# The seam between two stages of a fused spectral and graph convolution: who makes the low parts, and in which order

## The chip, the cores and the metric

The kernel runs on one core of a Trainium2 chip. The metric is the device time of one execution in microseconds; the median of a few executions is what is compared. The engines are TensorE (PE in the profile; PEld is its weight load), VectorE (DVE), ScalarE (ACT), GpSimd (POOL) and SyncE (SP), which here only issues transfers. ScalarE issues half of the transfers of the matrix. A `q` behind an engine's name in the profile means its queue, where transfers are issued.

## The reference

`x` is 4096 x 128 and `adj` is 4096 x 4096, both float32. `_layernorm` is a plain normalisation over the last axis.

```python
def _L0_gnn_ref(x, evals, evecs, t):              # evecs = adj
    t_eff = jnp.clip(t[0], 1e-08, None)
    x_spec = jnp.einsum('nk,nc->kc', evecs, x)
    coefs = jnp.exp(-evals * t_eff)[:, None]
    return jnp.einsum('nk,kc->nc', evecs, coefs * x_spec)

def _L1_gnn_ref(inputs, adj, W, b):
    adj_hat = adj + jnp.eye(N)
    deg = jnp.sum(adj_hat, axis=1, keepdims=True)
    return jnp.tanh((adj_hat / deg) @ (inputs @ W) + b)

x = _layernorm(x + _L0_gnn_ref(x, evals, adj, t), axis=-1)
x = _layernorm(x + _L1_gnn_ref(x, adj, W, b), axis=-1)
```

So the matrix is used three times: transposed for the spectrum, then for the spectral output, then for the graph product.

## The kernel before, in words

**Precision.** A product of two float32 tiles is made of three matmuls in float32r: each operand is split into a high part (a rounded copy) and a low part (the value less its high part), and high x high, high x low and low x high are summed in PSUM. Some products are instead made as one matmul in plain float32, called whole; such a step needs neither a high nor a low part of the matrix. Everywhere, ScalarE writes the high part (`hi`), and VectorE or GpSimd the low part (`lo`) by a subtraction.

**Stage 1, the spectrum (`visit1`, `chunk1`, `half1`).** The 4096 rows are eight groups of 512 (visits 0 to 7). A visit loads its rows in eight chunks `k`, each of two halves of 1024 columns, numbered `q` = 2k + h. Per half ScalarE makes `hi` (and row sums for the degrees, in `rsum`), VectorE `lo`, and TensorE does six matmuls. In the last visit (`LAST`), GpSimd makes the low parts of halves 1, 5, 9 and 13. `hi` and `lo` are rings of four slots here, six in the later stages. The eight PSUM banks hold the spectrum, and a bank pair is final after every fourth half of the last visit.

**The seam.** A bank pair `u` is copied by VectorE to `spec` (`spec_out`), turned by eight transposes on TensorE (`spectrum(u)`, `sT_done`), and scaled by `coef` as it is split. Before the change, for unit `k` (half a pair), ScalarE writes `s_hi` in four activations from PSUM, and for k of 4 and above two more that write `full`, a float32 copy of the unit's upper half; VectorE then writes `s_lo` in four operations from PSUM. `s_ready` counts the units that are done.

**Stage 2 and 3 (positions `p`).** The work is a list of 200 steps. A step is a load (2 MB, `n`), a unit, and one of two halves. The list is written by a planner: visit 0 is group 0 of the output, 16 steps from 4 loads, spectral products alone; visits 1 to 7 are the other groups, with graph products of the groups already known mixed in; visit 8 (steps from 134 on) is graph products alone. Each engine runs through the positions in the same order. At position p VectorE turns step p + 2 (`turn_step`, from the load buffer `raw` to `vt`), ScalarE makes `hi` of step p, GpSimd or VectorE `lo` of step p, and TensorE multiplies step p - 3 (`products`). `on_vector(s)` says which of the two makes a low part: in visits 0 to 2 every fourth split step goes to VectorE, in visit 8 every tenth, both by `SPLIT_COUNT`, the running number of split steps; in visits 3 to 7 it goes by the step's number. A slot of `hi`, `lo` and `vt` comes free when the step six before it is multiplied (`wait_slot`, `mm_done`).

**Loads.** There are four buffers (six in visit 8). The next load into a buffer is issued when the last step of its load is turned (`wait_buffer`, `BEFORE`): quarters 0 and 1 on SP's queue, quarters 2 and 3 on ScalarE's, where they are issued between its activations. SP also loads `x_sb` for each group, and moves the degrees out and back in (`deg_out`, `deg_in`) between two loads.

**Endings.** When a group is complete, `ending2` and `ending3` normalise it. They are spread over the next positions by `since2` and `since3`: among their pieces are `row_stats` and `mean_and_var` on VectorE and `inverse_deviation` on GpSimd, which stands in GpSimd's order between the low parts of two steps.

Of the kernel before, what the change touches and what calls it, by code (L numbers as in the profile page):

```python
# [27 lines left out]
def spectral_then_graph_conv(nc, x, adj, evals, t, W, b, out):  # L28
# [20 lines left out]
    R = 4  # L49
# [74 lines left out]
    def whole(s):  # L124

        st = STEP[s]
        return st.half == 1 and st.unit >= WHOLE_FROM and (st.visit < 3 and st.spectral or st.visit == NG)
# [16 lines left out]
    LATE_DVE = [q for q in range(PAIRS) if q % 4 != 1]  # L144

# [52 lines left out]
    with ctx:  # L198
# [22 lines left out]

        with nc.sbuf_tensor("xg_hi", [P, 2, R * C], f32r) as xg_hi, \
                nc.sbuf_tensor("xg_lo", [P, 2, R * C], f32r) as xg_lo, \
                nc.sbuf_tensor("spec", [P, 2, 2 * CW], f32) as spec, nc.sbuf_tensor("xn", [P, 2, R * C], f32) as xn, \
                nc.sbuf_tensor("rsum", [P, NG, R * NK], f32) as rsum:
# [34 lines left out]

        def acc2(g):
            return ps[:, g % 2, :]
# [28 lines left out]
        spec_out, sT_done, shi_ready, s_ready = map(sem, ("spec_out", "sT_done", "shi_ready", "s_ready"))  # L291
# [50 lines left out]
        def _(sp):  # L342
# [31 lines left out]
            for n in range(NL):  # L374
# [14 lines left out]
        def _(pool):  # L389
# [11 lines left out]
            for q in LATE_POOL:  # L401
# [4 lines left out]
                                        hi[:, q % RING1, :].bitcast(f32), ALU.subtract).then_inc(pool_lo1_ready, 1)  # L406

# [26 lines left out]
        def _(act):  # L434
# [55 lines left out]
            for i in range(NK + 4):  # L490
                if i < NK:
                    chunk1(LAST, i)
                if i >= 3 and i % 2 == 1 and i // 2 - 1 < NU:
                    wait_buffer(act, i // 2 - 1)
                    load_quarters(act, i // 2 - 1, (2, 3))
                if 0 <= (k := i - 4) < NK:
                    act.wait_ge(sT_done, k // 2 + 1)
                    if k == 0:
                        act.wait_ge(coef_ready, 1)
                    for jj in range(JB):  # L500
                        j = k * JB + jj
                        last = nc.scalar.activation(s_hi[:, j * C:(j + 1) * C], ps[:, k, jj * C:(jj + 1) * C],
                                                    ACT.Copy, scale=coef[:, k, jj:jj + 1])
                    if k >= WHOLE_FROM:
                        for jj in (2, 3):
# [392 lines left out]
```

## Time and profile before

| what | value |
|---|---|
| median of 3 runs | 627.07 us (626.67 to 628.39) |
| the profiled execution | 626.41 us, of which the span of the trace is 624.5 us |
| PE busy | 586.1 us, 94% of the span |
| DVE busy | 515.2 us, 82% |
| ACT busy | 400.6 us, 64% |
| POOL busy | 365.8 us, 59% |
| mean granted clock of TensorE | 0.981 |

Busy shares are means over stages with different limits. Matmuls overlap, so a busy TensorE is not one at its peak, and its idle stretches, or a granted clock under 1.00, are what costs. Stage 1 takes the first 194 us of the span, the seam runs from there to the first product at 206.1 us, and stages 2 and 3 take the rest.

### The profile page before, as it was taken

The numbers are of one execution on the slowest core, as the hardware profiler recorded it, in microseconds if no ns is written. First come the engines' busy times: TensorE is split into PE (matmuls) and PEld (weight loads), VectorE is DVE, ScalarE is ACT, GpSimd is POOL, SyncE is SP. The second block draws the span as 40 slices with busy tenths as digits, with TensorE's granted clock in tenths as the row PEclk, the third lists the DMA queues.
The fourth block names the chain that finished last, engine by engine and source line by source line (L and its number), as shares of the span: only waits on it lengthen the run. The fifth ranks groups of instructions, "written<-read, shape, count | busy, mean of one in ns | idle before, by whom it ended". The sixth has DMA issues, their size and how long they took to land.

```text
span 624.5 us, 8078 instructions
## 1 busy us (share of the span) xinstructions
PE 586.1 (94%) x2486; PEld 453.4 (73%) x2486; DVE 515.2 (82%) x605; ACT 400.6 (64%) x860; POOL 365.8 (59%) x210
## 2 busy tenths in 40 slices
PE   5999999999985799999999999999999979999993
PEld 5888888888874566667888888888888756656661
DVE  4899999999896999798889789597777586999992
ACT  4999999999975644545665646445454445544553
POOL 0000000000131988877999999779786879895972
PEclk9999999999998799999999999999999989999997
DMA  8999999999999899999996999387996299999201
GB/s 306 409 408 407 410 409 409 409 409 409 409 260 281 222 307 261 271 271 256 317 240 178 269 267 313 85 236 207 257 243 169 79 338 329 347 337 335 54 18 50
DMA packets 125065, 174.67 MB, mean 280 GB/s; under 512 B 6884, under 2 KB 105700, under 8 KB 125032
## 3 DMA queue, kind: packets, MB, share of 16 engines
q1 hardware_dynamic: 72608, 121.68, 59.5%
q10 hardware_dynamic: 52424, 52.58, 31.1%
q8 instruction: 17, 0.28, 0.2%
q14 instruction: 16, 0.13, 0.1%
HBM read 172.13 MB, written 2.11 MB: 279 GB/s over the span
## 4 chain that ended last, share of the span: by engine, by line
PE 78%; POOL 9%; DVE 5%; ACT 3%; issue 2%; ACTq 1%; DMA 1%; DVEq 0%
PE ps L785 13%; PE ps L787 13%; PE ps L786 13%; PE ps L761 9%; PE ps L762 9%; PE ps L763 9%; POOL lo L423 7%; PE ps L781 6%; DVE vt L616 3%; PE ps L850 1%; PE ps L853 1%; PE ps L746 1%; ACTq L336 1%; POOL rstd L415 1%; ACT hi L476 1%
## 5 line engine op out<-in xcount | busy, mean ns | idle before, releaser
L423 POOL TENSOR_TENSOR lo<-vt,hi 128x1024 fp32r<-128x1024 f32 x129 | 327.4, 2566 | 57.4 <-ACT hi L476 56.5
L616 DVE STREAM_TRANSPOSE vt<-raw 128x1024 f32<-128x1024 f32 x184 | 222.3, 1226 | 64.7 <-PE ps L787 54.4
L476 ACT ACTIVATE hi<-vt 128x1024 fp32r<-128x1024 f32 x163 | 169.8, 1061 | 110.3 <-DVE vt L616 91.8
L599 DVE TENSOR_TENSOR lo<-raw,hi 128x1024 fp32r<-128x1024 f32 x124 | 155.5, 1257 | 17.1 <-ACT hi L462 7.9
L462 ACT ACTIVATE hi<-raw 128x512 fp32r<-128x512 f32 x256 | 159.0, 624 | 5.4 <-PE ps L763 2.4
L404 POOL TENSOR_TENSOR lo<-raw,hi 128x1024 fp32r<-128x1024 f32 x4 | 10.7, 2674 | 177.0 <-ACT hi L462 177.0
L785 PE MATMUL ps<-hi,s_hi 128*128 128x512 f32 x232 | 99.0, 427 | 9.7 <-issue 5.2
L761 PE MATMUL ps<-hi,xg_hi 128*128 128x512 f32 x256 | 100.2, 392 | 2.4 <-DVE lo L599 1.8
L762 PE MATMUL ps<-lo,xg_hi 128*128 128x512 f32 x256 | 99.6, 389 | 0.0
L763 PE MATMUL ps<-hi,xg_lo 128*128 128x512 f32 x256 | 99.6, 389 | 0.0
L785 PE MATMUL ps<-hi,p_hi 128*128 128x512 f32 x206 | 89.1, 433 | 5.4 <-POOL lo L423 5.4
L786 PE MATMUL ps<-lo,s_hi 128*128 128x512 f32 x232 | 91.4, 394 | 0.0
L787 PE MATMUL ps<-hi,s_lo 128*128 128x512 f32 x232 | 91.4, 394 | 0.0
L787 PE MATMUL ps<-hi,p_lo 128*128 128x512 f32 x206 | 81.0, 393 | 0.0
L786 PE MATMUL ps<-lo,p_hi 128*128 128x512 f32 x206 | 80.9, 393 | 0.0
L781 PE MATMUL ps<-vt,full 128*128 128x512 f32 x148 | 69.5, 592 | 0.0
L623 DVE TENSOR_TENSOR lo<-vt,hi 128x1024 fp32r<-128x1024 f32 x34 | 65.3, 1920 | 1.6 <-ACT hi L476 1.6
L785 PEld LDWEIGHTS ps<-hi,s_hi 128*128 128x128 f32 x232 | 44.2, 190 | 26.1 <-issue 9.4
L761 PEld LDWEIGHTS ps<-hi,xg_hi 128*128 128x128 f32 x256 | 48.1, 188 | 13.9 <-DVE lo L599 2.3
L763 PEld LDWEIGHTS ps<-hi,xg_lo 128*128 128x128 f32 x256 | 48.1, 188 | 10.1
L762 PEld LDWEIGHTS ps<-lo,xg_hi 128*128 128x128 f32 x256 | 48.1, 188 | 9.6
L785 PEld LDWEIGHTS ps<-hi,p_hi 128*128 128x128 f32 x206 | 39.0, 189 | 21.0 <-POOL lo L423 10.2
(66 smaller groups left out, 515.9 us busy)
## 6 DMA issues: line engine op xcount, KB each, us to landing
raw<-in_adj_dram SPq DMA_DIRECT2D x63, 1024.0 KB, 14.7
raw<-in_adj_dram SPq DMA_DIRECT2D x90, 512.0 KB, 9.4
raw<-in_adj_dram ACTq DMA_DIRECT2D x88, 512.0 KB, 11.5
late_raw<-in_adj_dram SPq DMA_DIRECT2D x8, 512.0 KB, 11.3
late_raw<-in_adj_dram ACTq DMA_DIRECT2D x8, 512.0 KB, 13.5
xn<-in_x_dram SPq DMA_DIRECT2D x8, 256.0 KB, 14.4
x_sb<-in_x_dram SPq DMA_DIRECT2D x8, 256.0 KB, 13.3
out_dram<-x_sb ACTq DMA_DIRECT2D x7, 256.0 KB, 3.1
```

The source lines that it names most:

```text
L423: nc.gpsimd.tensor_tensor(lo[:, slot(p), :], vt[:, slot(p), :], hi[:, slot(p), :].bitcast(f32), ALU.subtract).then_inc(pool_lo_ready, 1)
L462: last = nc.scalar.activation(hi[:, q % RING1, e * CW:(e + 1) * CW], raw[:, k, 2 * h + e, :], ACT.Copy, accum_out=rsum[:, v, column:column ...
L476: nc.scalar.activation(hi[:, slot(s), :], vt[:, slot(s), :], ACT.Copy).then_inc(hi_ready, 1)
L599: nc.vector.tensor_tensor(lo[:, q % RING1, :], raw[:, k, 2 * h:2 * h + 2, :].rearrange("p r n -> p (r n)"), hi[:, q % RING1, :].bitcast(f3 ...
L616: nc.vector.transpose(vt[:, slot(s), :].rearrange("p (m a i) -> p m a i", m=2, a=RB), load_buffer(st.load).rearrange("p (a m e i) -> p e m ...
L761: nc.tensor.matmul(bank, xh, ah, start=first and r == 0, stop=False)
L762: nc.tensor.matmul(bank, xh, al, start=False, stop=False)
L763: last = nc.tensor.matmul(bank, xl, ah, start=False, stop=final and r == R - 1)
L781: return nc.tensor.matmul(out_t, full[:, STEP[s].unit - WHOLE_FROM, jj * C:(jj + 1) * C], vt[:, slot(s), jj * CW:(jj + 1) * CW], start=sta ...
L785: nc.tensor.matmul(out_t, vh, ah, start=start, stop=False)
L786: nc.tensor.matmul(out_t, vh, al, start=False, stop=False)
L787: return nc.tensor.matmul(out_t, vl, ah, start=False, stop=stop)
```

## The change

Seven edits, all at the seam or with an effect there:

1. `whole`: in visit 0 the second halves of all eight units are whole, not those of units 4 to 7 alone (steps 1, 3, 5 and 7 are new). This lowers `SPLIT_COUNT` of every later step by four, so in visit 8 the every-tenth rule falls on other steps: VectorE makes the low parts of steps 135, 147, 160 and 180, where it was 141, 156, 172 and 192. In visit 0 step 6 goes to VectorE, and steps 3 and 7 need no low part.
2. ScalarE's split of a unit (`split_spectrum`): four activations from PSUM write a float32 copy of the whole unit (`spectrum_full`), then one from that copy writes `s_hi`.
3. GpSimd makes `s_lo` (`spectrum_lo`) by one subtraction of 128 x 512 for each unit, from the copy and `s_hi`, in place of VectorE's four operations. Units 0 and 1 come ahead of half 13 of stage 1, units 2 and 3 ahead of step 0; units 4 to 7 after the low parts of positions 4, 6, 8 and 10, and ScalarE's splits of these units at the same positions.
4. VectorE turns steps 0 and 1 ahead of the copy of bank pair 2 (`spectrum_out(2)`), and step 2 ahead of pair 3.
5. TensorE does `spectrum(3)` after the products of steps 0 and 1, where it came ahead of all steps.
6. ScalarE's order at the end of stage 1 is written out: chunks 4 and 5 ahead of the first split, and the second quarters of loads 1 to 3 at other places.
7. `degrees()` runs at position 24 on VectorE, not at 8, and the two moves of the degrees on SP's queue stand one group of loads later.

```diff
-        return st.half == 1 and st.unit >= WHOLE_FROM and (st.visit < 3 and st.spectral or st.visit == NG)
+        if st.half == 0 or st.visit in range(3, NG):
+            return False
+        return st.visit == 0 or st.unit >= WHOLE_FROM and (st.spectral or st.visit == NG)
...
+    SPECTRUM_AFTER = {4: 4, 6: 5, 8: 6, 10: 7}
...
+        SF = {0: 0, 1: 1, 2: 2, 3: 3, 6: 4, 7: 0}
+        FULL_AT = {4: 0, 5: 1}
+        def spectrum_full(k):
+            if k in FULL_AT:
+                return full[:, 2 * FULL_AT[k]:2 * FULL_AT[k] + 2, :].rearrange("p a c -> p (a c)")
+            return sf[:, SF[k], :]
...
-                if n == 2 * NU - 1:
+                if n == 3 * NU - 1:
                     sp.wait_ge(deg_s, 3)
                     sp.dma_start(deg_by_tile, rdeg_tile[:, :, :]).then_inc(deg_out, 16)
-                if n == 3 * NU - 1:
+                if n == 4 * NU - 1:
...
+            def spectrum_lo(k):
+                pool.wait_ge(shi_ready, k + 1)
+                nc.gpsimd.tensor_tensor(s_lo[:, k * CW:(k + 1) * CW], spectrum_full(k),
+                                        s_hi[:, k * CW:(k + 1) * CW].bitcast(f32), ALU.subtract).then_inc(s_ready, 1)
+            assert LATE_POOL == [1, 5, 9, 13]
+            late_half(1)
+            late_half(5)
+            late_half(9)
+            spectrum_lo(0)
+            spectrum_lo(1)
+            late_half(13)
+            spectrum_lo(2)
+            spectrum_lo(3)
...
+                if p in SPECTRUM_AFTER:
+                    spectrum_lo(SPECTRUM_AFTER[p])
...
-            for i in range(NK + 4):
-                if i < NK:
...
+            def late_quarters(n):
+                wait_buffer(act, n)
+                load_quarters(act, n, (2, 3))
+            def split_spectrum(k):
+                act.wait_ge(sT_done, k // 2 + 1)
+                if k == 0:
+                    act.wait_ge(coef_ready, 1)
+                if k == LAST:
+                    act.wait_ge(mm_done, 2)
+                for jj in range(JB):
+                    last = nc.scalar.activation(spectrum_full(k)[:, jj * C:(jj + 1) * C], ps[:, k, jj * C:(jj + 1) * C],
+                                                ACT.Copy, scale=coef[:, k, jj:jj + 1])
+                last.then_inc(sfull_ready, 1)
+                act.wait_ge(sfull_ready, k + 1)
+                nc.scalar.activation(s_hi[:, k * CW:(k + 1) * CW], spectrum_full(k), ACT.Copy).then_inc(shi_ready, 1)
+            for k in range(NU):
+                chunk1(LAST, k)
+            late_quarters(0)
+            chunk1(LAST, 4)
+            chunk1(LAST, 5)
+            late_quarters(1)
+            split_spectrum(0)
+            split_spectrum(1)
+            chunk1(LAST, 6)
+            late_quarters(2)
+            chunk1(LAST, 7)
+            split_spectrum(2)
+            split_spectrum(3)
+            hi_step(0)
+            late_quarters(3)
+            hi_step(1)
...
+                if p in SPECTRUM_AFTER:
+                    split_spectrum(SPECTRUM_AFTER[p])
...
-            for i in range(NK + 4):
-                for h in range(2):
...
+            def spectrum_out(u):
+                dve.wait_ge(mm1_done, PAIRS * LAST + 4 * u + 4)
+                if u >= 2:
+                    dve.wait_ge(sT_done, u - 1)
+                for k in (2 * u, 2 * u + 1):
                     for e in range(2):
                         last = nc.vector.tensor_copy(
                             spec[:, u % 2, e * CW:(e + 1) * CW].rearrange("c (m q i) -> c q m i", m=JB, q=QN)
                             [:, 2 * (k % 2):2 * (k % 2) + 2],
                             ps[:, k, :].rearrange("c (q m e i) -> c e q m i", q=2, m=JB, e=2)[:, e])
-                    last.then_inc(spec_out, 1)
-                if 0 <= (k := i - 4) < NK:
...
+                last.then_inc(spec_out, 1)
+            for i in range(NK):
+                for h in range(2):
+                    if 2 * i + h in LATE_DVE:
+                        half1(LAST, i, h)
+                if i in (3, 5):
+                    spectrum_out((i - 3) // 2)
+            turn_step(0)
+            turn_step(1)
+            spectrum_out(2)
+            turn_step(2)
+            spectrum_out(3)
             turn_step(3)
...
-                if p == PAIRS // 2:
+                if p == PAIRS + PAIRS // 2:
...
-                    return nc.tensor.matmul(out_t, full[:, STEP[s].unit - WHOLE_FROM, jj * C:(jj + 1) * C],
+                    if STEP[s].spectral:
+                        columns_v = spectrum_full(STEP[s].unit)[:, 2 * C:]
+                    else:
+                        columns_v = full[:, STEP[s].unit - WHOLE_FROM, :]
+                    return nc.tensor.matmul(out_t, columns_v[:, jj * C:(jj + 1) * C],
...
-                    spectrum(k // 2 - 1)
-            spectrum(NU - 1)
...
+                if p - LAG == 1:
+                    spectrum(NU - 1)
```

## Rows read from the trace of the kernel before

**Rows 1.** Busy time by engine in four stretches (us), granted clock, DMA share, GB/s.
```profile
177.75:206.10 28.35, 16.51 (x81) 13.03 (x80) 23.13 (x52) 19.98 (x66) 7.08 (x3) 0.85 1.11 273
206.10:220.10 14.00, 11.36 (x37) 8.03 (x37) 13.93 (x15) 8.47 (x8) 13.88 (x6) 0.82 0.85 223
235.50:265.80 30.30, 28.95 (x118) 20.48 (x117) 25.38 (x29) 16.17 (x23) 25.91 (x14) 1.00 1.03 261
240.00:244.00 4.00, 4.00 (x18) 2.81 (x16) 4.00 (x8) 1.62 (x2) 2.92 (x2) 1.00 1.22 206
```

**Rows 2.** Timeline of TensorE at the seam: start, us, then idle before it.
```profile
180.16 0.50 PE L761 MATMUL ps<-hi,xg_hi 128*128 128x512 f32 x1 [1.36 <-DVE lo L599]
...
189.47 0.50 PE L761 MATMUL ps<-hi,xg_hi 128*128 128x512 f32 x1 [0.60 <-POOL lo L404]
...
198.97 0.47 PE L775 MATMUL ps<-ident,spec 128*128 128x128 f32 x1 [4.24 <-DVE spec L646]
...
206.11 0.76 PE L785 MATMUL ps<-hi,s_hi 128*128 128x512 f32 x1 [5.17 <-issue]
...
220.07 0.50 PE L785 MATMUL ps<-hi,s_hi 128*128 128x512 f32 x1 [1.66 <-POOL lo L423]
```

**Rows 3.** The chain that ended last, at the seam and in visit 0.
```profile
182.41 1.04 ACT s_hi L502 x4
183.45 2.44 ACT hi L462 x8
...
193.86 0.89 PE ps L775 x8
...
224.45 1.72 PE ps L781 x4
...
227.55 1.72 PE ps L781 x4
```

**Rows 4.** Groups by line: count, busy time and mean ns, idle before and releaser.
```profile
L423 POOL TENSOR_TENSOR lo<-vt,hi 128x1024 fp32r<-128x1024 f32 x129 | 327.4, 2566 | 57.4 <-ACT hi L476 56.5
L616 DVE STREAM_TRANSPOSE vt<-raw 128x1024 f32<-128x1024 f32 x184 | 222.3, 1226 | 64.7 <-PE ps L787 54.4 <-PE ps L781 10.0
L476 ACT ACTIVATE hi<-vt 128x1024 fp32r<-128x1024 f32 x163 | 169.8, 1061 | 110.3 <-DVE vt L616 91.8 <-PE ps L787 11.8 <-PE ps L781 3.2
L655 DVE SCALAR_TENSOR_TENSOR s_lo<-ps,coef,s_hi 128x128 fp32r<-128x128 f32 x32 | 9.0, 343 | 5.0 <-ACT full L506 4.2 <-ACT s_hi L502 0.8
L646 DVE COPY spec<-ps 128x256 f32<-128x256 f32 x16 | 5.6, 413 | 0.0
```

**Rows 5.** Timeline of GpSimd and of VectorE around 177 us.
```profile
176.64 2.38 POOL L404 TENSOR_TENSOR lo<-raw,hi 128x1024 fp32r<-128x1024 f32 x1 [3.16 <-ACT hi L462]
...
176.95 3.15 DVE L599 TENSOR_TENSOR lo<-raw,hi 128x1024 fp32r<-128x1024 f32 x1
```

**Rows 6.** Quarters 2 and 3 of loads 0 and 3: issue, and time to landing.
```profile
L336 ACTq DMA_DIRECT2D raw<-in_adj_dram x2: 338/422/505, 172.4 to 172.8; - x2
...
DMA to landing us min/median/max: 12.5/13.4/14.3
...
L336 ACTq DMA_DIRECT2D raw<-in_adj_dram x2: 318/415/512, 194.8 to 195.2; - x2
...
DMA to landing us min/median/max: 12.6/13.4/14.2
```

**Rows 7.** Timeline of TensorE and GpSimd in visit 8.
```profile
504.58 8.00 POOL L423 TENSOR_TENSOR lo<-vt,hi 128x1024 fp32r<-128x1024 f32 x3 [4.23 <-ACT hi L476]
...
507.00 0.50 PE L785 MATMUL ps<-hi,p_hi 128*128 128x512 f32 x1 [2.65 <-POOL lo L423]
...
516.64 0.50 PE L785 MATMUL ps<-hi,p_hi 128*128 128x512 f32 x1 [1.02 <-POOL lo L423]
...
580.28 0.20 POOL L412 TENSOR_TENSOR veps<-mv,eps_sb 128x4 f32<-128x4 f32 x1 [0.51 <-DVE mv L681]
...
584.38 0.50 PE L785 MATMUL ps<-hi,p_hi 128*128 128x512 f32 x1 [0.18 <-POOL lo L423]
```

More of the change, by code:

```diff
@@ L290, in spectral_then_graph_conv @@
         hi1_ready, lo1_ready, pool_lo1_ready, mm1_done = map(sem, ("hi1_ready", "lo1_ready", "pool_lo1_ready", "mm1_done"))
-        spec_out, sT_done, shi_ready, s_ready = map(sem, ("spec_out", "sT_done", "shi_ready", "s_ready"))
+        spec_out, sT_done, sfull_ready, shi_ready, s_ready = map(
+            sem, ("spec_out", "sT_done", "sfull_ready", "shi_ready", "s_ready"))
         vturned, hi_ready, lo_ready, pool_lo_ready, mm_done = map(
@@ L399, in _, with late_half @@
             pool.wait_ge(eps_ready, 1)
-            for q in LATE_POOL:
+            def late_half(q):
                 k, h = q // 2, q % 2
@@ L489, in _ @@
                 visit1(2 * d + 2, 0, d + 2)
-            for i in range(NK + 4):
-                if i < NK:
[L492 to L495, printed above, removed]
-                if 0 <= (k := i - 4) < NK:
[L497 to L505, printed above, removed]
-                            last = nc.scalar.activation(full[:, k - WHOLE_FROM, (jj - 2) * C:(jj - 1) * C],
-                                                        ps[:, k, jj * C:(jj + 1) * C], ACT.Copy,
-                                                        scale=coef[:, k, jj:jj + 1])
-                    last.then_inc(shi_ready, 1)
-                if i >= NK + 2:
-                    hi_step(i - NK - 2)
@@ L633, in _ @@
                 visit1(2 * d + 2, 0)
-            for i in range(NK + 4):
-                for h in range(2):
-                    if i < NK and 2 * i + h in LATE_DVE:
-                        half1(LAST, i, h)
-                for k in ((i - 3, i - 2) if i % 2 == 1 and 0 <= i - 3 < NK else ()):
-                    dve.wait_ge(mm1_done, PAIRS * LAST + 4 * (k // 2) + 4)
-                    u = k // 2
-                    if u >= 2:
-                        dve.wait_ge(sT_done, u - 1)
+            def spectrum_out(u):
[3 more added lines that the diff above has]
+                for k in (2 * u, 2 * u + 1):
                     for e in range(2):
@@ L649, in _ @@
                             ps[:, k, :].rearrange("c (q m e i) -> c e q m i", q=2, m=JB, e=2)[:, e])
-                    last.then_inc(spec_out, 1)
-                if 0 <= (k := i - 4) < NK:
-                    dve.wait_ge(shi_ready, k + 1)
-                    for jj in range(JB):
-                        j = k * JB + jj
-                        last = nc.vector.scalar_tensor_tensor(
-                            out=s_lo[:, j * C:(j + 1) * C], in0=ps[:, k, jj * C:(jj + 1) * C],
-                            scalar=coef[:, k, jj:jj + 1], in1=s_hi[:, j * C:(j + 1) * C].bitcast(f32),
-                            op0=ALU.mult, op1=ALU.subtract)
-                    last.then_inc(s_ready, 1)
-                if i >= NK + 1:
-                    turn_step(i - NK - 1)
+                last.then_inc(spec_out, 1)
[10 more added lines that the diff above has]
+            spectrum_out(3)
             turn_step(3)
-            assert not (whole(0) or on_vector(0) or whole(1) or on_vector(1))
+            assert not any(s in LO_BY_DVE for s in range(AHEAD))
             def degrees():
@@ L771, in spectrum @@
             def spectrum(u):
-                pe.wait_ge(spec_out, 2 * u + 2)
+                pe.wait_ge(spec_out, u + 1)
                 for c in range(2 * JB):
@@ L830, in _ @@
                 if k >= 3 and k % 2 == 1:
-                    spectrum(k // 2 - 1)
-            spectrum(NU - 1)
+                    spectrum((k - 3) // 2)
             def ending2(g, since):
```

2 lines of the change are left out of this document (1 added, 1 removed).

## The prediction, made before the change was run

> **What bounds the kernel now.** I read the busy time by stretch first: it shows where TensorE, busy 94% of the span, is not. From 177.75 to 220.10 it is busy 27.87 of 42.35 us [rows 1]: 14.5 us idle, and a granted clock of 0.85 and 0.82 on top. In the visit behind it is idle 1.35 of 30.30 us. So the seam is the one large hole. The timeline of TensorE then names what ends each gap [rows 2]: low parts of stage 1 (1.36 and 0.60 us), the copy of bank pair 3 behind VectorE's `s_lo` (4.24 us), the first low part of step 0 (5.17 us, put down to issue, though GpSimd finishes just then), and in visit 0 GpSimd (1.66 us). The first product after the 5.17 us takes 0.76 us, that after the 1.66 us 0.50 us: the long idle stretch brought TensorE to the lower of its clock levels (1.2 GHz), the short one did not. Last I read GpSimd, transfers and visit 8, since an earlier start presses on them.
>
> **Prices.** A split step or half is six matmuls: the pair of a whole and a split step recurs after 3.10 us and the whole one takes 1.72, so 1.38 is left [rows 3]. Eight transposes take 0.89, four activations from PSUM 1.04, a chunk of two halves on ScalarE 2.44 [rows 3]. A turn is 1.2, `hi` 1.04, VectorE's `s_lo` of a unit 4 x 9.0/32 = 1.1, the copy of a bank pair 4 x 5.6/16 = 1.4 [rows 4]. GpSimd's low part of 1024 columns is 2.38 when nothing disturbs it [rows 5] and 2.57 in the mean [rows 4]. Its 512-column one does not occur before: above 0.2 (128x4, [rows 7]) and below 2.38; it is half the columns, so 1.2. ScalarE's copy of 512 columns from SBUF lies between 0.5 (half of `hi`) and 1.04; with its wait for the activations ahead of it I take 0.65, so a split is 1.7.
>
> **The walk to step 0 (edits 2 to 6).** Half 8 starts at 180.16 in either kernel: VectorE's low part for it took 3.15 us in place of about 1.2, because it lay beside GpSimd's half 9 [rows 5], and both stay. Chunk 5 now fills ScalarE's idle time ahead of the first split; the two new copies take that up again, so chunk 6 still starts near 183.4. TensorE: halves 8 to 11 to 185.7, transposes to 186.6, half 12 to 188.0 with no wait; half 13's `hi` is there at 185.9, GpSimd starts when VectorE's half 12 is done (186.1) and ends 188.5, a wait of 0.5; halves 13 to 15 end at 192.6, against 189.47 + 3 x 1.38 = 193.6 now [rows 2]. VectorE: halves 14 and 15 behind GpSimd's 13, to 190.9; the two turns that are moved ahead of the copy, to 193.2; the copy of pair 2, to 194.6. TensorE thus waits 2.05 us there, a wait that the moved turns create, and ends its transposes at 195.5. Meanwhile ScalarE ends chunk 7 at 189.0, splits 2 and 3 at 192.4, `hi` of step 0 at 193.4; GpSimd's two unit lows end at 193.5 beside it, and its low part of step 0 at 195.95. Step 0 starts at 196.0 in place of 206.11.
>
> The Trainium skill (GPSIMD Engine Reference, Key points) says that GpSimd shares its SBUF interfaces with VectorE and contends with instructions of two SBUF inputs. The trace agrees by its 3.15 us. It speaks against handing more subtractions to GpSimd; I let the two wait for each other wherever they meet above.
>
> **Visit 0 (edits 1, 3, 5).** Sixteen steps are now eight pairs of 3.10, with 0.89 for the last transposes: 25.7 us. The four new whole steps cost TensorE 4 x 0.34 = 1.4, and spare GpSimd three low parts, VectorE one (and hand it step 6). GpSimd then has from 195.95: five low parts of 2.38 and four unit lows of 1.2, 16.7 us, and about 4 us in which it waits for `hi`, a split or VectorE; step 12 is ready at 216.6, as TensorE comes to it. I count two waits of 0.5. The visit ends at 196.0 + 25.7 + 1.0 = 222.7. Now it ends after the whole step at 227.55 and two more pairs, 227.55 + 1.72 + 6.20 = 235.5 [rows 3]. The difference is -12.8 us.
>
> **What is given back.**
> - Clock. The 2.05 us wait lies between 1.66 (kept) and 5.17 (lost) [rows 2]. Lost, it costs 0.18 x 14.0 = 2.5 [rows 1], less what the waits for GpSimd absorb. Half of that, less this: +0.8 (0 to 2.5).
> - Transfers. ScalarE's quarters of load 0 landed at 187.1, of load 3 at 209.4 [rows 6]: 7.4 us a load with the queues never empty. Load 3 comes some 0.9 earlier, at 208.5, and load n at 208.5 + 7.4(n-3). A step needs its load 4.7 us ahead of its products (turn, `hi`, low part). Step 20 would run at 228.2 and needs load 5 at 223.5; it lands at 223.3. Load 6 is needed at 230.1 and lands at 230.7. A visit is 30.3 long [rows 1], so step 44 would run near 274.2 and needs load 11 at 269.5; it lands at 267.7. All just in time: +1.0 (0 to 3). Behind visit 2 each step has more products, and this ends.
> - Degrees. 1.5 us on VectorE (estimate: three small operations, each under the 1.2 of a turn) go from position 8, where GpSimd is the bound, to 24, where VectorE is full (4.00 of 4.00 us) [rows 1]. They stand behind the statistics of group 0, ahead of the low part of step 26: +0.4 (0 to 1.5). The moves on SP's queue only change places: 0.
> - Visit 8. By the new count step 141 goes to GpSimd. Its queue there is 138, 139, 140 in 8.00 from 504.58, then the ending's small chain, then 142, which TensorE waits for at 516.64 [rows 7]. Four low parts undisturbed are 9.52, the chain 1.65, the next 2.38: 518.15, so +1.5. Step 147's move to VectorE relieves GpSimd only behind that. Step 180 goes to VectorE directly ahead of the statistics for which `inverse_deviation` already waits at 580.28; step 182's low part stands behind that, and TensorE for it at 584.38 [rows 7]: +1.2. Step 160 stands likewise ahead of the first row's statistics, but saves GpSimd one low part just there: +0.5. Steps 135, 156, 172 and 192 change where GpSimd or VectorE has idle time: 0; without that cover each is one low part, at most 2.4. Sum +3.2 (0 to 6).
>
> Visits 3 to 7 only shift.
>
> **Sum.** 626.41 (this execution) - 12.8 + 0.8 + 1.0 + 0.4 + 3.2 = 619.0. The median shown is 0.66 above its profiled execution: 619.7. About 1.9 us, 0.3%, is what a measurement of this kernel can tell from no change.
>
> **Rivals.**
> - All of the gain is kept: 614.3. For it: TensorE has idle time of its own in visit 8, which could be late at no price. Against: both steps in question are ones it waits for. 0.15.
> - The 512-column low part costs more. At 2.2 units 2 and 3 put step 0 off by 1.7 and step 12 comes 2.4 late in place of 0: 622.1. For it, only that a size not seen is guessed; against, the cost per column of the same operation. 0.08. The Trainium skill (GPSIMD Engine Reference, Key points) says that elementwise work is about twice as fast on VectorE; twice `s_lo`'s 1.1 would be 2.2, while twice a subtraction of 1.2 for 1024 columns fits the 2.38.
> - Transfers become the bound in visits 1 and 2. At 8.0 us a load, load 11 lands at 272.5, 3 late in place of 1: 622 to 623. 2.1 MB at the 206 GB/s of 240 to 244 is 10.2, at 261 it is 8.0 [rows 1]. 0.16.
> - The other side, slower: the same mechanism further on. Load 11 at 269.5 + 12.8 takes the whole gain, which is 9.2 us a load; with the rest given back it decides at 8.7. At 9.5 load 11 lands 15.0 late: 634. For it, the 206 GB/s; against, that stretch held the degrees' and `x_sb`'s transfers, and 7.4 is measured over three whole loads. 0.06.
> - The walk fails and step 0 starts past 202: 625 to 628. 0.07.
>
> The forecast has 0.48, its own range 617 to 622. With the rivals the range is 614 to 625. Faster: forecast, all kept, dear low parts, late transfers but the worst, 0.84; same 0.09; slower 0.07.
>
> **What would show it.** Step 0's product near 196, with one idle stretch near 2 us ahead of it; the first `stage` copy of group 0 near 222.7; GpSimd's 512-column operation near 1.2; VectorE waiting for a transfer ahead of the turns of steps 20 to 44, or not; TensorE's waits ahead of steps 142 and 182, 1.5 and 1.2 longer. It is wrong if the clock falls at 192.6 and stays down, if loads come slower than 7.6 us apart, or if visit 8 waits elsewhere.

## The result, and the profile after

The changed kernel takes **618.84 us** (median of 4 executions, 617.27 to 618.94) where the kernel before takes 626.87 (4, 625.44 to 628.39): a ratio of 0.9887 on record, 95% interval 0.9866 to 0.9907 (the quotient of the two medians, 0.9872, lies in it). The forecast was 619.7. The profiled execution took 618.76 us with a span of 616.8, against the sum's 619.0.

Busy time by stretch of the changed kernel (seam, visit 0, visit 1, then from the copy of group 7 to the end), columns as in [rows 1]:

```profile
179.22:194.30 15.08, 13.47 (x64) 10.57 (x65) 14.32 (x17) 11.85 (x35) 11.71 (x6) 1.00 1.11 332
194.30:222.49 28.19, 27.72 (x94) 16.66 (x94) 26.61 (x26) 17.63 (x32) 21.73 (x11) 1.00 1.10 333
222.49:252.85 30.36, 28.48 (x113) 20.05 (x114) 23.98 (x32) 16.30 (x24) 26.57 (x15) 1.00 0.98 294
484.23:616.80 132.57, 112.07 (x400) 71.86 (x398) 103.25 (x179) 62.19 (x97) 96.55 (x75) 0.96 0.77 217
```

From half 8 to the copy of group 0 the changed kernel takes 43.27 us, of which TensorE is idle 2.08, at a granted clock of 1.00 throughout. Between the same two points the kernel before takes 55.35 us, of which TensorE is idle 13.12, at a granted clock of 0.88 in the mean:

```profile
180.16:235.51 55.35, 42.23 (x161) 30.32 (x162) 48.30 (x76) 33.50 (x77) 32.10 (x13) 0.88 1.05 275
```

So 11.0 of the 12.1 us are idle time that is gone, and 1.0 is busy time, in which the clock and the four new whole steps pull opposite ways.

The changed kernel's timeline, with the rows that answer to [rows 2, 3]:

```profile
179.22 0.50 PE L807 MATMUL ps<-hi,xg_hi 128*128 128x512 f32 x1 [1.38 <-DVE lo L647]
...
193.11 1.09 PE L821 MATMUL ps<-ident,spec 128*128 128x128 f32 x8 [1.43 <-DVE spec L690]
...
214.37 0.50 PE L835 MATMUL ps<-hi,s_hi 128*128 128x512 f32 x1 [0.21 <-POOL lo L455]
...
218.97 1.88 PE L831 MATMUL ps<-vt,sf 128*128 128x512 f32 x4
...
222.61 0.50 PE L835 MATMUL ps<-hi,s_hi 128*128 128x512 f32 x1 [0.37 <-POOL lo L455]
...
225.93 0.50 PE L835 MATMUL ps<-hi,s_hi 128*128 128x512 f32 x1 [1.18 <-POOL lo L455]
```

The 4.24 and the 5.17 us are gone. One wait of 1.43 stands in their place, ahead of the transposes of pair 2, step 0 runs directly behind them at 194.30, and visit 0's last whole step starts at 218.97 (before 233.59). GpSimd's low parts of the units:

```profile
180.11 1.35 POOL L427 TENSOR_TENSOR s_lo<-sf,s_hi 128x512 fp32r<-128x512 f32 x1 [2.02 <-ACT s_hi L540]
181.81 1.90 POOL L427 TENSOR_TENSOR s_lo<-sf,s_hi 128x512 fp32r<-128x512 f32 x1 [0.35 <-ACT s_hi L540]
...
207.11 1.30 POOL L427 TENSOR_TENSOR s_lo<-sf,s_hi 128x512 fp32r<-128x512 f32 x1
```

1.30 us undisturbed, where 1.2 was assumed. The rows at 180.11 and 181.81 lie on either side of a low part on VectorE:

```profile
180.23 2.31 DVE L647 TENSOR_TENSOR lo<-raw,hi 128x1024 fp32r<-128x1024 f32 x1
```

GpSimd's first one began 0.12 us ahead of it and took 1.35, close to its undisturbed time; VectorE's took 2.31 where 1.2 is usual, and ended 1.08 us after GpSimd's had. GpSimd's next one began inside VectorE's and took 1.90, ending 1.17 us after it. So here the two take turns, and the one that starts second pays. The same holds for the 3.15 us of [rows 5]: GpSimd's began first and kept its 2.38.

The whole span by checkpoints, the starts of ScalarE's copy to `stage` of a finished group (it waits for the group's last product):

| us | half 8 | group 0 | group 1 | group 2 | group 7 | group 7 to the end of the span |
|---|---|---|---|---|---|---|
| before | 180.16 | 235.51 | 266.17 | 301.20 | 497.52 | 126.98 |
| after | 179.22 | 222.49 | 252.85 | 287.89 | 484.23 | 132.57 |
| difference | -0.94 | -13.02 | -13.32 | -13.31 | -13.29 | +5.59 |

The 0.94 us ahead of half 8 lies in a stage that the change barely touches, and this start differs from execution to execution: it is 178.43 to 180.01 us in the variants below that have the new seam, and 179.70 in the one with the old. So copies are best compared from half 8. From there the seam gained 12.1 us at group 0 and 12.4 at groups 1 and 7, and visit 8 gave 5.6 back. One more measure of noise is needed below: seven kernels (the changed one and six variants) are the same code up to group 7, and from half 8 to the copy of group 0 their traces take 42.27 to 43.58 us, to that of group 1 73.23 to 74.19.

In visit 8 TensorE and its suppliers look like this, to be set beside [rows 7]:

```profile
494.19 0.50 PE L835 MATMUL ps<-hi,p_hi 128*128 128x512 f32 x1 [3.14 <-POOL lo L455]
...
505.20 0.50 PE L835 MATMUL ps<-hi,p_hi 128*128 128x512 f32 x1 [2.31 <-POOL lo L455]
...
542.28 0.50 PE L835 MATMUL ps<-hi,p_hi 128*128 128x512 f32 x1 [1.58 <-POOL lo L455]
549.62 0.50 PE L835 MATMUL ps<-hi,p_hi 128*128 128x512 f32 x1 [0.86 <-POOL lo L455]
576.71 0.50 PE L835 MATMUL ps<-hi,p_hi 128*128 128x512 f32 x1 [0.35 <-POOL lo L455]
```

```profile
491.77 9.41 POOL L455 TENSOR_TENSOR lo<-vt,hi 128x1024 fp32r<-128x1024 f32 x4 [5.89 <-ACT hi L510]
...
538.21 0.20 POOL L444 TENSOR_TENSOR veps<-mv,eps_sb 128x4 f32<-128x4 f32 x1 [2.38 <-DVE mv L727]
...
572.62 0.20 POOL L444 TENSOR_TENSOR veps<-mv,eps_sb 128x4 f32<-128x4 f32 x1 [3.26 <-DVE mv L727]
```

GpSimd now has four low parts in a row (x4, 9.41) where it had three (x3, 8.00), and then the ending's chain. It waits 2.38 and 3.26 us for the mean (`mv`), since VectorE has a low part of its own directly ahead of the statistics. The first of the two:

```profile
534.28 2.63 DVE L671 TENSOR_TENSOR lo<-vt,hi 128x1024 fp32r<-128x1024 f32 x1
536.84 0.88 DVE L721 BATCH_NORM_STATS2 stats<-ps 128x6 f32<-128x128 f32 x4
537.75 0.38 DVE L727 BATCH_NORM_AGGREGATE mv<-stats 128x2 f32<-128x6 f32 x4
```

### The profile page after: what moved, and what is told of

The parts are those of the page before. It is cut to its first block, busy times and chain, and to the rows that moved or that the text cites. A ratio compares the mean times of both kernels' runs of the same rounds, so it can differ in the third digit from the quotient of the medians.

```text
span 616.8 us, 8026 instructions
## 1 busy us (share of the span) xinstructions
PE 584.1 (95%) x2478; PEld 448.7 (73%) x2478; DVE 509.7 (83%) x572; ACT 398.4 (65%) x856; POOL 366.6 (59%) x215
## 4 chain that ended last, share of the span: by engine, by line
PE 79%; DVE 8%; POOL 6%; ACT 2%; ACTq 2%; issue 2%; DMA 1%; DVEq 0%
PE ps L835 14%; PE ps L837 13%; PE ps L836 13%; PE ps L807 9%; PE ps L809 9%; PE ps L808 9%; PE ps L831 7%; POOL lo L455 5%; DVE vt L664 3%; ACTq L353 2%; DVE lo L647 1%; PE ps L898 1%; PE ps L901 1%; PE ps L792 1%; POOL rstd L447 1%
## 5 line engine op out<-in xcount | busy, mean ns | idle before, releaser
L455 POOL TENSOR_TENSOR lo<-vt,hi 128x1024 fp32r<-128x1024 f32 x126 | 317.1, 2541 | 46.8 <-ACT hi L510 46.2
L510 ACT ACTIVATE hi<-vt 128x1024 fp32r<-128x1024 f32 x159 | 165.1, 1060 | 105.9 <-DVE vt L664 87.9
L647 DVE TENSOR_TENSOR lo<-raw,hi 128x1024 fp32r<-128x1024 f32 x124 | 157.6, 1276 | 16.9 <-ACT hi L496 8.7
L835 PE MATMUL ps<-hi,s_hi 128*128 128x512 f32 x224 | 95.1, 425 | 3.1 <-POOL lo L455 2.6
L837 PE MATMUL ps<-hi,s_lo 128*128 128x512 f32 x224 | 87.5, 391 | 0.0
L836 PE MATMUL ps<-lo,s_hi 128*128 128x512 f32 x224 | 87.4, 390 | 0.0
L671 DVE TENSOR_TENSOR lo<-vt,hi 128x1024 fp32r<-128x1024 f32 x33 | 67.1, 2034 | 0.0
L831 PE MATMUL ps<-vt,full 128*128 128x512 f32 x124 | 59.1, 600 | 0.0
L835 PEld LDWEIGHTS ps<-hi,s_hi 128*128 128x128 f32 x224 | 42.1, 188 | 19.7 <-POOL lo L455 8.1
## 6 DMA issues: line engine op xcount, KB each, us to landing
x_sb<-in_x_dram SPq DMA_DIRECT2D x8, 256.0 KB, 13.7
```

What stands on the lines that cost most here:

```text
L510: nc.scalar.activation(hi[:, slot(s), :], vt[:, slot(s), :], ACT.Copy).then_inc(hi_ready, 1)
L647: nc.vector.tensor_tensor(lo[:, q % RING1, :], raw[:, k, 2 * h:2 * h + 2, :].rearrange("p r n -> p (r n)"), hi[:, q % RING1, :].bitcast(f3 ...
L831: return nc.tensor.matmul(out_t, columns_v[:, jj * C:(jj + 1) * C], vt[:, slot(s), jj * CW:(jj + 1) * CW], start=start, stop=stop)
L835: nc.tensor.matmul(out_t, vh, ah, start=start, stop=False)
L836: nc.tensor.matmul(out_t, vh, al, start=False, stop=False)
L837: return nc.tensor.matmul(out_t, vl, ah, start=False, stop=stop)
```

## The experiments

Twelve variants, all timed beside the kernel before. Its medians on the four occasions were 625.03, 625.27, 625.05 and 625.15 us. Most variants start from the changed kernel with VectorE's steps of visit 8 put back to 141, 156, 172, 192, called **base** below; the steps are given by this line, `SPLIT_COUNT[s] % 10 == 0` in both kernels:

```diff
-            return SPLIT_COUNT[s] % 10 == 0
+            return s in (141, 156, 172, 192)
```

**1. Who makes which low part of visit 8.** The base, from the changed kernel:

> The changed kernel, but in visit 8 VectorE makes the low parts of steps 141, 156, 172 and 192 again, as in the kernel before. Theory: the 5.6 us that the changed kernel loses again behind group 7 come from the new deal of low parts, and the lower clock after 505 us from the longer wait that it makes there; then 613.0 to 614.5 us, and the copies of groups 0 to 7 unchanged. Rival 1: they come from the changed phase of the transfers that ScalarE issues at 486 us; then 617 us or more. Rival 2: only the two waits that were forecast (1.5 and 1.2 us) go: 616 us.

Median 615.25 us (5 executions, 612.28 to 615.9), ratio 0.9828 (0.9800 to 0.9856). Group 0's copy is at 222.41 as in the changed kernel, and group 7 to the end takes 129.24 us in place of 132.57: 3.3 of the 5.6 us come back. The time lies between the theory's range and the rival's 616. It spreads, too: two of the five executions took 612.28 and 613.14, two to three microseconds less than the one that was profiled, so 3.3 is a low figure. Three variants below that have the same deal and issue their transfers at the same places in this stretch take 128.0 to 128.2 us there, which is 4.4 to 4.6 back.

The same by itself: the kernel before, its seam untouched, with the steps of the changed kernel (135, 147, 160, 180):

> The kernel before, with only its deal of low parts in visit 8 changed to steps 135, 147, 160 and 180. Theory: the deal alone costs 4.5 to 6 us wherever the seam lies: 631.5 to 633 us. Rival: it costs that only with the changed kernel's phase of transfers: 627 to 629 us.

Median 631.76 (4, 629.97 to 631.84), ratio 1.0099 (1.0074 to 1.0124). Group 7 is at 497.10, as before, and the rest takes 132.9 us in place of 126.98. So the new deal alone costs 5.9 us where nothing else is changed, as the theory had it. TensorE waits 2.31 us for step 142, the very wait of the changed kernel, and 1.66 us at the row behind step 160.

A deal that puts VectorE's parts early, `s in (139, 141, 156, 158)`, from the changed kernel:

> The changed kernel, but in visit 8 VectorE makes the low parts of steps 139, 141, 156 and 158. Theory: GpSimd reaches the ending's small chain and step 142 one low part earlier than with the old deal, and step 162's low part waits for no other: 2 to 3 us under deal_old, 611 to 612.5 us. Rival: VectorE's low part 139 waits for GpSimd's 138 and the gain is under 0.5 us.

Median 616.89 (4, 616.54 to 617.71), ratio 0.9875 (0.9853 to 0.9897): far from the 611 to 612.5 expected, and no better than the base. With one low part fewer ahead of the ending GpSimd is through at 497.6, but the mean comes only at 500.5, and TensorE then waits 2.74 us at 504.62 for what follows the chain:

```profile
500.54 0.20 POOL L444 TENSOR_TENSOR veps<-mv,eps_sb 128x4 f32<-128x4 f32 x1 [2.90 <-DVE mv L727]
```

In the base VectorE's part of step 141 stands directly ahead of `mean_and_var` as well, but there GpSimd is busy until 499.71, and the mean (497.43 to 497.80) is early. So what counts is not whether statistics stand behind VectorE's part, but whether they still come before GpSimd has done its own parts.

A deal read off the waits that were left, `s in (138, 142, 148, 158, 172)`, five parts and not four, from the changed kernel:

> The changed kernel with VectorE's parts at steps 138, 142, 148, 158, 172, loads issued as in it. Theory (where VectorE takes over decides, and it is best early and spread): 611.5 to 614, copy of group 7 to the end 127 to 129. Rival (the hold of ScalarE sets the first wait whatever VectorE does): 614.5 to 616, as with the steps 141, 156, 172, 192.

Median 614.32 (5, 614.15 to 614.75), ratio 0.9826 (0.9809 to 0.9843), group 7 to the end 127.5 us. Step 138 waits for VectorE, and a microsecond less:

```profile
494.30 0.80 PE L835 MATMUL ps<-hi,p_hi 128*128 128x512 f32 x1 [2.05 <-DVE lo L671]
```

The stretch behind group 7 is as expected; the time lies just above the theory's range and just below the rival's. It is steady: its five executions lie within 0.6 us, the base's within 3.6. The two ratios' intervals overlap, so that it is faster than the base is not shown.

**2. What the whole steps of visit 0 are worth.** From the changed kernel:

```diff
-        return st.visit == 0 or st.unit >= WHOLE_FROM and (st.spectral or st.visit == NG)
+        return st.unit >= WHOLE_FROM and (st.spectral or st.visit == NG)
```

> The changed kernel, but in visit 0 only the second halves of units 4 to 7 are whole, which brings the old deal of visit 8 back as well. To be read beside deal_old. Theory: GpSimd then has seven low parts of 2.4 us in visit 0 besides four unit lows of 1.3 us and bounds the visit, which ends 3 to 5 us later: 617 to 618.5 us. Rival: GpSimd has room, and TensorE saves 4 x 0.34 us: 612.3 us.

Median 616.35 (4, 616.31 to 616.4), ratio 0.9862 (0.9841 to 0.9883). With half as many whole steps TensorE waits for GpSimd seven times in visit 0, 5.6 us in sum, the longest

```profile
205.61 0.50 PE L835 MATMUL ps<-hi,s_hi 128*128 128x512 f32 x1 [1.93 <-POOL lo L455]
```

and group 0 is copied at 226.21, 3.7 us later, or 47.31 us from half 8 where the seven kernels take 42.27 to 43.58. The mechanism is the expected one; the time is a little under its range, for the following reason. `SPLIT_COUNT` runs over the whole list, so four more split steps at its start put visit 8's deal back by themselves, as expected, and visit 8 is shorter than thought: the end comes 2.3 us earlier than in the changed kernel. The four whole steps of visit 0 gain 3.7 us there, and between group 7 and the end the kernel that has them is 6.2 us longer (132.57 against 126.35). Over half of that is the shift of a counter: the old deal has 3.3 of it back in the base, 4.4 to 4.6 in the three variants with its deal. With the deal fixed, as in the base, the medians are 1.1 us apart (615.25 and 616.35), and the ratios' intervals overlap: that the new whole steps gain anything at the end is not shown by these two.

**3. Who makes the spectrum's low parts.** The base, with the eight low parts on VectorE from the same float32 copies, each at the place in VectorE's order where the copy is ready (`spectrum_lo(k)` moved from GpSimd's program to VectorE's):

> The kernel of deal_old, but VectorE makes the eight 512-column low parts, from the same copy: units 0 and 1 behind half 12, 2 and 3 behind the turn of step 3, 4 to 7 at positions 4, 6, 8 and 10. Theory: units 2 and 3 no longer stand ahead of step 0's low part on GpSimd, so step 0's low part starts no later than 191.8 us, and unit 0's is ready in time; the copy of group 0 comes within 1 us of 222.4 us, since TensorE and not GpSimd bounds visit 0. Rival: VectorE, with its turns behind those waits, bounds the visit, and the copy comes 2 to 5 us later.

Median 618.95 (4, 618.16 to 620.1), ratio 0.9901 (0.9879 to 0.9922). The theory fell and the rival held: group 0 is copied at 225.80, 3.1 us later net of the start of half 8, and groups 1 and 7 are 4.3 us later, net as well. TensorE waits in visit 0 for either engine's low parts, where the base has no wait between 194.69 and 214.65:

```profile
204.68 0.50 PE L841 MATMUL ps<-hi,s_hi 128*128 128x512 f32 x1 [2.10 <-POOL lo L451]
208.61 0.50 PE L841 MATMUL ps<-hi,s_hi 128*128 128x512 f32 x1 [0.56 <-DVE lo L665]
```

So with the rest of the new seam in place, having GpSimd and not VectorE make these low parts is worth 3 to 4 us; this is a low part made from the copy on either engine, not the four operations from PSUM of the kernel before. Experiment 2 puts the whole steps at about 4 of the 12 us in the same way. The rest (the turns and the last pair moved, ScalarE's order, the float32 copy that frees the banks) was not taken apart by a run.

**4. The last pair ahead of step 0.** The base, with `spectrum(3)` in TensorE's program ahead of all steps and not behind step 1:

> The kernel of deal_old, with the transposes of bank pair 3 ahead of step 0 again. Their copy ends at 195.4 us on VectorE. Theory: TensorE waits for it, starts step 0 at 196.4 instead of 194.3 us, and the clock falls in the wait; the copy of group 0 comes 2 to 4 us later. Rival: GpSimd is late by as much anyhow, and it comes under 0.7 us later.

Median 613.91 (4, 612.36 to 615.52), ratio 0.9812 (0.9786 to 0.9837). The theory's second wait comes, and the clock falls with it (0.81 granted from 191 to 200 us, the eight transposes take 1.97 us where the eight ahead of them took 1.09):

```profile
192.96 1.09 PE L821 MATMUL ps<-ident,spec 128*128 128x128 f32 x8 [1.43 <-DVE spec L690]
195.41 1.97 PE L821 MATMUL ps<-ident,spec 128*128 128x128 f32 x8 [1.36 <-DVE spec L690]
```

Yet group 0 is copied only 0.46 us later, not 2 to 4; from half 8 it is 0.90 (43.80 against the base's 42.90), just outside the 42.27 to 43.58 of the seven kernels. The total is no worse. From step 0 at 197.02 TensorE has no wait until 235.98, where the base waits 0.20 us at 194.69 (put down to issue) and, for GpSimd, 0.21 at 214.65 and 1.19 at 225.87: the loss falls mostly into time that was waited for low parts anyway.

**5. The degrees at their old place.** The base, with `degrees()` at position 8 and its transfers one visit earlier:

```diff
-                if p == PAIRS + PAIRS // 2:
+                if p == PAIRS // 2:
                     degrees()
```

> The kernel of deal_old, with the degrees at position 8 again and their transfers one group of loads earlier. The prediction took 0.4 us for the degrees at position 24 and found loads just in time in visits 1 and 2. Theory now: VectorE and the loads have room at both places, so the copies of groups 0 and 1 stay within 0.5 us of 222.4 and 252.8 us. Rival: the small packets of the degrees hold the loads of visit 1 up, and the copies of groups 1 and 2 come 1 to 4 us later.

Median 615.58 (4, 614.94 to 616.03), ratio 0.9844 (0.9824 to 0.9864). Group 0 is where it was (222.34), groups 1 and 2 are 1.1 us later than in the base (253.84, 288.92), and that is still there at group 7 (485.21 against 484.16). But from half 8 group 1 takes 74.42 us, 0.2 above what kernels of identical code take (73.23, the base's 73.27, up to 74.19). So a cost of the old place is not shown, at group 1 or in the total.

**6. ScalarE's hold behind group 7.** The first two low parts of visit 8 wait for `hi`, and ScalarE is late because it issues four quarters of the two loads into the extra buffers directly behind the copy of group 7:

```profile
484.23 0.60 ACT L569 ACTIVATE stage<-ps 128x512 f32<-128x512 f32 x1 [2.96 <-PE ps L837]
484.24 6.29 ACTq L353 DMA_DIRECT2D late_raw<-in_adj_dram  x4
490.63 1.06 ACT L510 ACTIVATE hi<-vt 128x1024 fp32r<-128x1024 f32 x1 [5.81 <-PE ps L837]
```

The idle time is put down to TensorE, but the queue's own row fills it: four issues take 6.29 us, and `hi` runs as they end. I tried to put them four positions later, when the group's ending is past:

```diff
-                if p == END2[LAST] + LAG + 1:
+                if p == END2[LAST] + LAG + 5:
```

> The kernel of deal_old, with ScalarE's quarters of the two loads into the extra buffers issued four positions later (position 141, not 137). Theory: ScalarE's queue is held for 6.3 us there while the transfers ahead drain, so step 138 comes 3.2 us late and the clock falls in most executions; both go, and the time is 608.5 to 611 us with little spread. Rival: ScalarE is held as long at the new place, and another step comes late: 613 to 616 us, spread as before. The copy of group 7 stays at 484.2 us.

Median 620.11 (6, 619.25 to 621.31), ratio 0.9919 (0.9902 to 0.9936), above the rival's 613 to 616 too: my theory fell. Step 138 is no longer late (0.43 us at 494.47), but the hold became longer, and TensorE's wait with it:

```profile
490.65 11.83 ACTq L353 DMA_DIRECT2D late_raw<-in_adj_dram  x4
502.58 1.06 ACT L510 ACTIVATE hi<-vt 128x1024 fp32r<-128x1024 f32 x1 [12.10 <-issue]
```

```profile
506.11 0.80 PE L835 MATMUL ps<-hi,p_hi 128*128 128x512 f32 x1 [8.60 <-POOL lo L455]
```

Then without ScalarE, the base with all four quarters of these two loads on SyncE's queue:

```diff
-                load_quarters(sp, n, (0, 1))
+                extra = LOADS[n].buf >= BUFS and BEFORE[n] is None
+                load_quarters(sp, n, (0, 1, 2, 3) if extra else (0, 1))
```

> The kernel with VectorE's parts of visit 8 at steps 141, 156, 172, 192, in which SyncE and not ScalarE issues all four quarters of the two loads into the extra buffers. Theory (ScalarE is held about 6 us behind group 7's end by the queue it fills with the four quarters, so its two squares at step 138 come late, TensorE waits 3.2 us there and in some executions loses its clock): ScalarE has no hold behind group 7's copy, step 138 waits under 1.5 us, the clock behind group 7 stays at .94 or more; copy of group 7 to the end 125.5 to 127 us instead of 129.2, time 609 to 612. Rival (the hold is the price of the transfers themselves: SyncE's own queue is held instead, the loads land later, and the first inverses or the stores wait for it): 613 to 616.

Median 617.81 (613.13 to 624.09, 6 executions; the ratio is of the five up to 619.34), ratio 0.9869 (0.9837 to 0.9902), where the theory had 609 to 612 and the rival 613 to 616. Half of the theory held: ScalarE's `hi` follows the copy at 487.32, step 138 doesn't wait, and from 484 to 494 TensorE is busy 9.56 of 10 us where the base has 6.98. The rival took it back. VectorE waits for the very loads that were moved:

```profile
523.52 3.50 DVE L660 STREAM_TRANSPOSE vt<-late_raw 128x1024 f32<-128x1024 f32 x3 [7.33 <-DMA late_raw<-in_adj_dram]
```

and the two kernels' stretches from 494 to 514, of this variant and then of the base, differ in what the transfers bring:

```profile
494.00:514.00 20.00, 17.53 (x67) 12.55 (x66) 13.69 (x17) 9.40 (x17) 17.60 (x11) 0.91 1.12 238
```

```profile
494.00:514.00 20.00, 18.88 (x66) 13.06 (x67) 13.33 (x14) 10.87 (x18) 19.84 (x13) 0.84 1.11 342
```

238 GB/s against 342 at nearly the same DMA share. That the hold is the price of having both queues carry the loads fits this; the runs show the rates, not the reason for them. Nor is a low rate tied to the one queue: the changed kernel, with both in use, has 215 GB/s at a share of 1.11 from 514.23 to 524.23. The same with the deal of `deal2`, `s in (138, 142, 148, 158, 172)`:

> The same with VectorE's parts at steps 138, 142, 148, 158, 172 (five of the visit's parts instead of four). Theory: the first wait of visit 8 is GpSimd's part at step 138 (1.2 us later than VectorE's would be) and the one at 142 the chain of the last mean; with both on VectorE the copy of group 7 to the end falls to 124 to 126 us, time 607.5 to 610.5. Rival (VectorE's parts delay the mean behind group 7, or the clock and the transfers set this stretch): no better than the kernel with SyncE's loads alone, 610 to 614.

Median 616.09 (4, 614.4 to 617.36), ratio 0.9861 (0.9840 to 0.9882), above the 614.32 of that deal with ScalarE's issues left alone, and the expected 607.5 to 610.5 was missed by far. VectorE waits 8.84 us for `late_raw` at 522.20.

**7. The two best edits together**, the deal of `deal2` and the last pair ahead of step 0:

> The changed kernel with VectorE's parts of visit 8 at steps 138, 142, 148, 158, 172 and the last pair of spectrum units turned ahead of step 0, the two edits that did best one by one. Theory (the two act in stretches 300 us apart; the turn ahead of step 0 costs at most 0.9 us, and the loss of the clock there is hidden behind GpSimd): 613 to 615, the same as with the steps alone. Rival (the earlier last pair lets units 6 and 7 come early and takes a wait out of visit 0, which the noise of its first run hid): 611.5 to 613, copy of group 0 below 222.

Median 613.90 (5, 612.8 to 614.47), ratio 0.9817 (0.9803 to 0.9831), group 0 copied at 222.13. The theory held: no more than the deal by itself (614.32), within what five executions tell apart. Group 0's copy is that early only because half 8 started at 178.43; from there it takes 43.70 us, with 43.58 for the deal alone. With experiment 4 it has the lowest median of the thirteen, 1.8% under the kernel before, and 0.7% under the changed kernel going by the ratios; the intervals of the four lowest overlap.

## Why the prediction was right, point by point

**Step 0 at 196.0.** It ran at 194.30, or 195.24 with the 0.94 us put back. The wait that the moved turns create ahead of pair 2's transposes was there as forecast, 1.43 and not 2.05 us. The walk's order (which engine waits for which) held at each step that the trace shows.

**Visit 0.** From step 0 to the end of the last whole step (218.97 + 1.72 = 220.69) it took 26.4 us; 26.7 was forecast. The eight pairs were right, and of the two waits of 0.5 there was one of 0.21. So TensorE had ended the visit 14.6 us earlier than before (235.31), 13.7 net of the 0.94; -12.8 was forecast. The copy of group 0 says less, 13.0, because ScalarE was still in its issues:

```profile
219.54 2.91 ACTq L353 DMA_DIRECT2D raw<-in_adj_dram  x1
222.49 0.60 ACT L569 ACTIVATE stage<-ps 128x512 f32<-128x512 f32 x1 [1.92 <-PE ps L837]
```

**The clock, +0.8.** Nothing: 1.00 granted through the seam. The 1.43 us wait is shorter than the 1.66 that kept it before [rows 2]. Experiment 4 shows the case that was feared, with two such waits in 2.5 us, and that it cost 0.5 to 0.9 us at group 0.

**Transfers, +1.0.** Near in size (1.3), wrong in place, so the size is luck. The loads kept up: between 178 and 484 us VectorE waited for a transfer once, 0.44 us at 212.68. What an earlier seam pressed on was the issuing engine. ScalarE stood 4.29 us in two issues from 212.28 and 2.91 us in one from 219.54, its `hi` came late, GpSimd idled 3.48 us ahead of 217.80, and TensorE waited 0.37 and 1.18 us behind visit 0: that is how 14.6 us became 13.3.

**Degrees, +0.4.** Nothing visible, and experiment 5 does not show a difference between the two places either. VectorE's three operations took 0.9 us at 232.17, where 1.5 was assumed.

**Visit 8, +3.2.** The mechanism was right and the size short: 5.6. From the copy of group 7, by TensorE's rows:
- Step 138 comes 9.96 us behind the copy, 9.48 before: 0.5 that was in no term. It is not the deal's, since the base has 9.99 and the kernel before with the new deal 9.42. It goes with ScalarE's hold, 6.29 us where it was 5.53. The hold is 5.45 to 5.53 in the three kernels without the new whole steps of visit 0, and 6.14 to 6.39 in the eight that have them and issue at this place.
- From step 138 to step 142, 11.01 us in place of 9.64: +1.4, where +1.5 was forecast, and 11.00 with the deal alone.
- From 142 to the third whole step behind it (522.20, before 532.23), 17.0 in place of 15.6: +1.4 that was in no term. The granted clock says how. These are ten microseconds about step 142 (516.64 before, 505.20 after), of the kernel before and then of the changed one:

```profile
507.00:517.00 10.00, 8.07 (x26) 5.48 (x27) 8.13 (x9) 4.91 (x8) 9.84 (x8) 0.83 1.10 347
```

```profile
504.20:514.20 10.00, 9.00 (x32) 6.04 (x33) 4.74 (x3) 4.38 (x10) 7.97 (x4) 0.83 1.09 334
```

  Both lose 0.17 of their clock. Before, the loss fell ahead of step 142 (0.50 granted from 509 to 511 us, the lower level, 1.2 GHz), where TensorE waited for GpSimd anyway; now it falls behind it (0.50 from 507.2 to 509.2), where TensorE has work to do, and 0.17 x 10 is 1.7, an estimate. Two variants bear it out. The kernel before with the new deal has 0.83 granted behind step 142 and takes 16.8 us to the same whole step. The variant of experiment 3, with the old deal, kept 1.00 on both sides, and took 9.66 us from step 138 to 142 and 15.6 from there: no less than the kernel before, so the clock lost ahead of step 142 costs nothing.
- Around step 160, from the fifth whole step to the eleventh (528.89 to 558.01, before 538.91 to 565.85), +2.2 where +0.5 was forecast. This is the term that was mis-sized. VectorE's low part took 2.63 us beside GpSimd's, not 1.2; the statistics came that much later, GpSimd waited 2.38 for them, and TensorE then 1.58 and 0.86. I had taken the low part saved on GpSimd as making up for it.
- Steps 180 and 182: the wait for the mean was there (3.26 on GpSimd), but TensorE's was 0.35 where it was 0.18 [rows 7]. +0.2, where +1.2 was forecast.

These five pieces add up to 5.7, against 5.59 from checkpoint to end.

The sum: -12.8 + 0.8 + 1.0 + 0.4 + 3.2 = -7.4 forecast. Measured, -13.3 + 5.6 = -7.7. That the time came out within 1 us is luck, because two errors nearly cancel: the visits 0 to 7 kept 2.7 us more than forecast, 0.94 of it no doing of the change as far as the traces tell, and visit 8 gave 2.4 more back.

**Rivals.** "All kept" (614.3) fell: the two steps named were waited for. It is about where the kernel lands once the deal is put right (614.3 to 615.3), which shows how much hung on that counter. "Dear low parts" fell, 1.30 us and not 2.2, but 1.2 was low too. "Transfers the bound" and its far end fell for visits 1 and 2; it is what happened when I took one queue away (experiment 6). "The walk fails" fell.

**Open.** Why visit 8 takes longer with the new seam than with the old, the deal being the same: 129.24 us in the base, 128.0 to 128.2 in the variants of experiments 3, 4 and 5, 126.98 in the kernel before. In the base it is 2.3. 0.5 is step 138's. TensorE's waits for GpSimd behind it are no longer, 2.4 us in sum where they were 2.7. 0.9 lies between the third and the seventh whole step (519.40 to 540.89, before 532.23 to 552.81), with a granted clock of 1.00 in both; it is in the base's trace alone (20.6 to 20.7 us in the three variants, 20.6 before, 21.5 in the base). The rest comes behind that. Nor is it shown what sets the length of ScalarE's hold, or why experiment 2's visit 8, whose seam is new but for the whole steps, is as short as the kernel before's: both go with the whole steps of visit 0, and no run says how.

## What to carry to other kernels

When work is dealt out by a counter over a whole list, an edit at the front reshuffles the far end: here four whole steps more in visit 0 changed who makes which low part 300 us further on, and that stretch gave back over 40% of the gain. So fix the far end's deal by name, then time the edit. A low part directly ahead of the statistics of an ending holds up three engines when the mean then comes after GpSimd is free (steps 160 and 180 here), and nobody when it does not (step 141 in the base). So count what stands behind each one you move, not its own length. Before you move a transfer's issue off a busy engine, ask which queues then carry the bytes: the time that the issuer is held may be what keeps both queues full (the rates here fit that, they do not prove it).

## What the runs showed of the hardware

- An engine that issues transfers is held, and the hold is not a constant: four quarters of 512 KB held ScalarE 6.29 us when issued at 484.24, 11.83 us when issued at 490.65 in the late variant. The idle time that follows is put down in the timeline to another engine; the rows of the queue tell it.
- At a DMA share of 1.11 to 1.12 the same matrix came at 342 GB/s with the loads spread over SyncE's and ScalarE's queues, and at 238 with two of them on SyncE's alone; the changed kernel had 215 at 1.11 from 514.23 to 524.23 with both queues in use. The DMA share does not tell the rate.
- A stretch of the clock's lower level was a matter of place and run: in the changed kernel the 3.14 us wait at 494.19 was followed by a product of 0.50 us and 1.00 granted for ten microseconds, in the base the 3.17 us wait at 494.15 by one of 0.79 us and 0.70 granted. The base's executions came at 612.3 and 613.1 us with mean clocks of 0.995 and 0.991, and at 615.3 to 615.9 with 0.988. The Trainium skill (TensorE: Matmul & The Clock Gate, Part 1) says of the clock's rise that it varies between runs of one kernel. The mean clocks of the five executions differ, which fits; only one of them has a trace, so the moment itself is not compared here.
- Of two subtractions that meet, the one that starts second pays, and the first keeps its time. VectorE's 1024 columns took 1.18 us alone and 2.63 when started inside GpSimd's, whose four took 9.45 us, 2.36 each; GpSimd's 512 columns took 1.30 alone, 1.90 when started inside VectorE's, and 1.35 when started 0.12 us ahead of it.
